# A ring of five half one-hots and four id fields in a recommender tower

## The reference, cut to what matters

```python
e = jnp.stack([tbl_0[ids[:, 0]], ..., tbl_25[ids[:, 25]]], axis=1)
combined = jnp.concatenate([dense[:, None, :], e], axis=1)          # 2048 x 27 x 128
inter = jnp.einsum('bfd,bgd->bfg', combined, combined)[:, iu, ju]   # pairs f < g
h = jnp.concatenate([dense, inter, dense], axis=1)
h = jnp.maximum(h @ W_top1 + b_top1, 0.0)     # 607 x 512
h = jnp.maximum(h @ W_top2 + b_top2, 0.0)     # 512 x 256
y = h @ W_top3                                # 256 x 1
```

## Time and profile before

| what | value |
|---|---|
| median of three runs | 360.73 us |
| the profiled execution | 359.68 us |
| its span on the core | 357.9 us |
| TensorE matmuls busy | 324.8 us (91%) |
| VectorE busy | 240.9 us (67%) |
| ScalarE busy | 183.4 us (51%) |
| GpSimd busy | 250.5 us (70%) |
| granted TensorE clock, mean | 0.986 |

### The profile page before, as it was taken

One profiled execution on the slowest core, in us unless ns is written; L12 is line 12 of the kernel. 1 busy time (PEld: TensorE's weight loads), 2 busy tenths in 40 slices (PEclk: granted clock), 3 DMA queues, 4 the chain that ended last, 5 costly groups with the idle time before them and its releaser, 6 DMA issues.

```text
span 357.9 us, 10386 instructions
## 1 busy us (share of the span) xinstructions
PE 324.8 (91%) x4192; PEld 312.4 (87%) x4192; DVE 240.9 (67%) x721; ACT 183.4 (51%) x359; POOL 250.5 (70%) x268
## 2 busy tenths in 40 slices
PE   0565779999999999999999999999999999998966
PEld 0464679999999999999899999999899999997955
DVE  3999976996479663995299555986199547941011
ACT  2345455457534763557544664457345763376224
POOL 4777777777777777777777777777777777774310
PEclk9999989999999999999999999999999999999889
DMA  7999577573457424652456344642466335521220
GB/s 184 259 233 228 139 218 198 121 192 82 98 110 192 95 75 107 162 145 71 100 124 183 88 97 98 164 132 70 104 142 170 77 103 108 123 66 38 43 69 0
DMA packets 47470, 44.80 MB, mean 125 GB/s; under 512 B 26139, under 2 KB 41499, under 8 KB 47423
## 3 DMA queue, kind: packets, MB, share of 16 engines
q1 hardware_dynamic: 37946, 25.90, 30.4%
q0 software_dynamic: 8448, 17.04, 19.3%
q10 hardware_dynamic: 1028, 1.20, 1.2%
HBM read 39.33 MB, written 4.78 MB: 123 GB/s over the span
## 4 chain that ended last, share of the span: by engine, by line
PE 56%; POOL 18%; DVE 9%; DMA 7%; issue 7%; SPq 1%; ACT 1%; ACTq 0%
PE ps_o L330 28%; POOL rows L309 18%; PE ps_m L367 10%; PE ps_g L356 9%; DVE onehot L719 6%; PE ps_t L341 5%; DVE tbl_lo L704 3%; DMA oh_ids<-onehot_ids 2%; PE ps_m L395 1%; DMA x<-interaction_scratch 1%; DMA interaction_scratch<-inter 1%; DMA b2s<-b 1%; DMA x<-w_pairs 1%; DMA rows<-tables,idx 1%; PE ps_o L410 1%
## 5 line engine op out<-in xcount | busy, mean ns | idle before, releaser
L309 POOL DMA_INDIRECT rows<-tables,idx x256 | 245.6, 959 | 81.5 <-issue 76.5
L719 DVE TENSOR_SCALAR onehot<-oh_ids,rownum 125x256 fp32r<-125x256 int32 x640 | 200.4, 388 | 51.7 <-PE ps_o L330 46.6
L330 PE MATMUL ps_o<-onehot,tbl_hi 125*128 125x256 f32 x640 | 160.5, 291 | 22.5 <-DVE tbl_lo L704 22.0
L330 PE MATMUL ps_o<-onehot,tbl_lo 125*128 125x256 f32 x640 | 156.3, 284 | 0.0
L330 PEld LDWEIGHTS ps_o<-onehot,tbl_hi 125*128 125x128 f32 x640 | 123.3, 193 | 27.1 <-DVE tbl_lo L704 23.9
L330 PEld LDWEIGHTS ps_o<-onehot,tbl_lo 125*128 125x128 f32 x640 | 123.7, 193 | 0.0
L533 ACT ACTIVATE emb<-ps_o 128x256 f32<-128x256 f32 x80 | 49.3, 740 | 90.0 <-PE ps_o L330 86.9
L356 PEld LDWEIGHTS ps_g<-emb 128*54 128x54 f32 x2048 | 56.6, 136 | 4.9 <-issue 2.6
L356 PE MATMUL ps_g<-emb 128*54 128x54 f32 x2048 | 58.9, 220 | 2.0 <-issue 1.3
L549 ACT ACTIVATE emb<-ps_t 128x512 f32<-128x512 f32 x64 | 46.4, 727 | 8.2 <-PE ps_t L341 7.9
L564 ACT ACTIVATE inter<-ps_g 128x432 f32<-128x432 f32 x64 | 34.0, 531 | 18.5 <-PE ps_g L356 16.4
(11 more groups left out here) (55 smaller groups left out, 207.5 us busy)
## 6 DMA issues: line engine op xcount, KB each, us to landing
oh_ids<-onehot_ids SPq DMA_DIRECT2D x80, 128.0 KB
rows<-tables,idx POOLq DMA_INDIRECT x256
x<-interaction_scratch SPq DMA_DIRECT2D x24, 117.0 KB
inter<-small_tables SPq DMA_DIRECT2D x4, 448.0 KB
interaction_scratch<-inter SPq DMA_DIRECT2D x30, 47.2 KB
interaction_scratch<-inter SPq DMA_DIRECT2D x28, 42.2 KB
interaction_scratch<-inter SPq DMA_DIRECT2D x30, 38.2 KB
dense<-dense_e SPq DMA_DIRECT2D x8, 128.0 KB
```

The lines of the kernel that those rows point to most:

```text
L309: pool.indirect_dma_start(rows[e][:, k, :], None, tables[k], bass.IndirectOffsetOnAxis(ap=idx[:, NG * hh + k:NG * hh + k + 1], axis=0),).t ...
L330: mm = pe.matmul(o, tbl[p][:, k, c, :], onehot[n % SLOTS_OH][:, c, :], start=(c + p == 0), stop=(c == TCHUNKS - 1 and p == 1))
L719: op = nc.vector.tensor_scalar(onehot[n % SLOTS_OH][:, c, :], oh_ids[0:TPART, n % IDS, :], rownum[:, c:c + 1], None, ALU.is_equal)
```

## The change

The three whole one-hots become a ring of five half one-hots (`RING = 5`): half `g = 2n + c // PART` lies in slot `g % 5`. VectorE waits before each half until `onehot_used` is at least `g - 4`, that is until the half five places earlier is used; before it was the half six places earlier. The id slots go from six to four, so `load_ids(n)` waits for one-hot `n-4` instead of `n-6`. SP's list is changed with it: in the first block `load_ids(n)` stands behind `load_stage(n)` where it was `load_ids(n+2)`, and for each later block fields 0 to 6 are asked for ahead and fields 7, 8 and 9 between the stores and `load_x`; before it was fields 0 to 8 ahead and field 9 there.

```diff
-    SLOTS_OH = 3
-    IDS = 6
+    RING = 5
+    IDS = 4
...
-        onehot = [sb(f"onehot{s}", [TPART, TCHUNKS, BLOCK], f32r) for s in range(SLOTS_OH)]
+        onehot = [sb(f"onehot{s}", [TPART, PART, BLOCK], f32r) for s in range(RING)]
...
                 store_wrapped(sp, i, range(QUAD), inter_stored)
-                load_ids(NO * (i + 1) + NO - 1)
+                for n in range(7, NO):
+                    load_ids(NO * (i + 1) + n)
                 for c in range(PAIR_CHUNKS):
                     load_x(sp, i, c)
...
             load_dense(0)
-            load_ids(4)
-            load_ids(5)
-            load_stage(sp, 4)
-            load_ids(6)
             load_idx(1, 2 * NG, HALVES * NG)
-            for n in range(5, NO):
+            for n in range(4, NO):
                 load_stage(sp, n)
-                load_ids(n + 2)
+                load_ids(n)
             load_dense(1)
             for n in range(NO, ITEMS):
                 load_stage(sp, n)
-                load_ids(n + 2)
+                load_ids(n)
...
-            for n in range(ITEMS + 2, 2 * NO - 1):
+            for n in range(ITEMS, NO + 7):
                 load_ids(n)
...
-                    for n in range(NO * (i + 1), NO * (i + 2) - 1):
+                    for n in range(NO * (i + 1), NO * (i + 1) + 7):
                         load_ids(n)
...
# lookup (TensorE)
+                    g = 2 * n + c // PART
-                        pe.wait_ge(onehot_ready, 2 * n + c // PART + 1)
+                        pe.wait_ge(onehot_ready, g + 1)
-                        mm = pe.matmul(o, tbl[p][:, k, c, :], onehot[n % SLOTS_OH][:, c, :],
+                        mm = pe.matmul(o, tbl[p][:, k, c, :], onehot[g % RING][:, c % PART, :],
...
# make_onehot (VectorE)
+                    g = 2 * n + c // PART
-                        wait(dve, onehot_used, 2 * (n - SLOTS_OH) + c // PART + 1)
-                    op = nc.vector.tensor_scalar(onehot[n % SLOTS_OH][:, c, :], oh_ids[0:TPART, n % IDS, :],
+                        wait(dve, onehot_used, g - RING + 1)
+                    op = nc.vector.tensor_scalar(onehot[g % RING][:, c % PART, :], oh_ids[0:TPART, n % IDS, :],
```

## The result

The changed kernel takes a median of 384.67 us (four runs, 383.64 to 386.43) against 360.22 for the kernel before: 1.069 times as long, 95% interval 1.063 to 1.074. The profiled execution took 386.43 us, with a span of 384.6 where it was 357.9: 26.7 us more. It is the slowest of the four.

The account below looks back on a forecast made before the run. TensorE was taken to bound blocks 1 to 6, GpSimd's fixed gather pace as second bound. Terms 2.6 (first block), 2.3 (block 1), 13.2 (blocks 2 to 7) sum to 18.1, less 0.8: 17.3 on 359.68, 377.0 us; range 363 to 387.

Parts of the forecast that it names:

- the chain: Blocks 2 to 7: ring delays one-hot 2, SP's stores wait behind field 6's ids, field 7's ids come late; 13.2 us.
- the free 0.8: At the end TensorE is ready about 0.8 us before the last gather; that much delay is free, subtracted from the sum.
- The ids' landing: Field 7's ids, behind the stores, land 2.7 us after issue; VectorE stalls 2.03 us in a block like 2.
- rival 4: The landing is late, 3.6 us or a little more: stall 2.9 to 3.6, 383 to 387 us; chance 0.12.
- The ring in the blocks: Blocks like 2: 60 chunks left after TensorE's first half lookup; by itself some 0.04 us a block, whole margin gone.
- Block 1: Block 1: restart 60.99, field 7's ids land at 74.6, wanted at 74.0; end 82.15 against 79.87, 2.3 us.
- The ring in the first block: First block: second one-hot halves wait for lookups; 1.05 us at one-hot 2 plus 1.5, all 2.6 reach block 1.
- The seven of 0.22: First block, one-hots 3 to 9: VectorE's fifth chunk 0.22 us late each, seven times, 1.5 us.
- The first block's ids: First 10 us: two id loads of 128 KB leave; gain 0, at most 0.1 us.
- rival 2: The clock falls too after TensorE's waits, 1.7 us lost seven times: 12 more, 389 us; chance 0.10.
- rival 3: GpSimd's pace hides the loss, gathers end at 327.5 whatever TensorE does; time stays 359.7 us; chance 0.07.

Follow-up runs that it names:

- two moves in SP's list and two in VectorE's: Changed kernel with field 6's load behind eighth store, first block's ids ahead of tables, split_lo(k) between one-hot halves, dense weight split before one-hot 12's ring wait: 359.69 us.

## Why the prediction was right, and where its terms were off
The direction, the place and the chain were right: 377.0 was forecast, 384.67 came, inside the range of 363 to 387. The rows show each link, and the chain was cut by experiments in three places (which one-hot the load waits for, where it stands, when field 7's ids are issued).

The sum was too small in every stretch of the kernel. In the profiled execution 17.3 us were forecast and 26.7 came: 4.5 for 2.6 at the start of block 1, 3.1 for 2.3 in block 1, 16.7 for 11.0 in blocks 2 to 6, and 2.5 for 1.4 in block 7 with the tail (2.2 less the free 0.8).

**The ids' landing** was the largest error of size. I took 2.7 us from the stores; the id loads of blocks 2 to 7 behind the stores took 3.3 to 3.8 (3.57 in block 2). The row that I took it from the earlier trace rows is of four stores in the tail that GpSimd issues; the trace has no landing of a store from SP's queue, so the price came from another queue. Four stores of `L197`, also issued by GpSimd in the tail, took 3.0 to 4.4 us. That is rival 4 (0.12; 383 to 387 us), the forecast's mechanism with the landing of the upper rows, and the time that came lies in its range. In part that is luck: 7 of the missing 9.4 us are in blocks 2 to 7, the rest is other terms. Issue was forecast 11.9 us after the block's first lookup and was 11.5 to 12.8, later in some blocks. So the stall was 2.6 to 4.0 us and not 2.0. "DMA: Bandwidth & Descriptors" of the Trainium skill ("Anatomy of one DMA") would have made it 2.3, an estimate by a fit for DMAs issued from GpSimd; the trace does not agree for SP's, and says 3.3 or more for this load in this place.

**The ring in the blocks** was right for blocks 2 to 4: with the ring alone they are 39.4 to 39.6 us. Blocks 5 and 6 of that run were 40.8 and 40.3, through waits for gathered rows of which the prediction knew nothing.

**Block 1** was forecast 2.3 us longer and was 3.1. VectorE waited 1.08 us for ids and not 0.7, and restarted 1.58 us after the block's start, for 1.33 before. I had also put the time at which lookup 9's ninth matmul is wanted at 79.87; it starts at 79.71. The wait of SP's dense load for the dense weights was not in my reckoning at all; it decides once field 6 is out of the way.

**The ring in the first block** was too dear: 2.6 forecast, 0.7 to 1.0 measured in VectorE's list. The wait at one-hot 2 was there (0.98 for 1.05). The seven of 0.22 were not: VectorE's eight chunks take 2.64 us with the short ring and took 2.63 before. I reckoned its fifth chunk from the mean pace, though the row itself was longer than eight such paces; the chunks already had a pause of about that size in these places. What makes that pause was not tried.

**The first block's ids** failed as a step. I wrote that two loads leave the first 10 us and costed the rest at nothing. But fields 4 to 13 were also moved further back among the table loads (`load_ids(n)` behind table n, where it was `load_ids(n + 2)`), and I did not ask when they land. They landed too late four times:

```profile
37.67 2.54 DVE L718 TENSOR_SCALAR onehot<-oh_ids,rownum 125x256 fp32r<-125x256 int32 x8 [0.54 <-DMA oh_ids<-onehot_ids]
...
49.52 2.54 DVE L718 TENSOR_SCALAR onehot<-oh_ids,rownum 125x256 fp32r<-125x256 int32 x8 [3.41 <-DMA oh_ids<-onehot_ids]
```

The last row, field 0 of block 1, comes partly in place of a wait of 1.64 us for weights. By the first weight split the list is 3.6 us behind, and the bias load that releases block 1 landed after 5.57 us where it took 3.75: 4.5 us in all. So the 2.6 for the start of block 1 had one term too large and one missing; the surplus of the one covered part of the other by luck.

**The clock** (rival 2, 0.10) came true in part. I held that the wait would be spread over six halves; it is one wait at lookup 7's first half, as VectorE makes the later halves almost as fast as TensorE wants them. After 1.32 to 1.6 us of it the clock stayed (blocks 2, 4, 6), after 1.90 and 2.4 it fell (blocks 3, 5, 7), with 0.83 granted in the 10 us around it. The length of the wait does not decide it alone: in the run with the ids ahead of the tables it stayed after 2.14 us and fell after 1.92. "TensorE: Matmul & The Clock Gate" ("HAM oscillation") of the Trainium skill describes such rounds, and the trace agrees in every second block. (Block 1's 0.96 follows a wait of 2.4 us for the biases at its start.) The price was not 1.7 us but what a block has beyond VectorE's wait: 43.41 - 39.42 - 3.2 = 0.8 in block 3, 43.82 - 39.42 - 3.9 = 0.5 in block 5.

**Not slower** (rival 3) is out: the 0.8 us of waiting for the last gather was used up. But its premise, that the gathers end at 327.5 whatever TensorE does, did not hold: the last one started 3.1 us later in the changed kernel and 5.4 later with the ring alone.

## What to carry to other kernels
A queue that issues DMAs in order is a lock: shrinking a buffer is cheap or dear by what stands behind the load that now waits, and by who consumes the last thing in that list. Two cuts that cost 3.5 us each can cost 24 together, when one makes an event late and the other puts an urgent transfer behind it. Before shrinking a ring, list for every slot wait the event that frees it, and move from behind it what does not need it; here two moves in SP's list and two in VectorE's gave all of it back. Taking away the wait that decides can bring up the next one in the same list: here the dense load's, which had been almost hidden behind field 6's.

## What was not expected of the hardware
The same 128 KB id load took 2.9 to 7.7 us to land where the trace has it, and was never as quick as the median (2.6) of the four stores of `L188` that GpSimd issues in the tail; 7.5 and 7.7 were behind table loads in the first block. In the changed kernel the clock stayed after waits of up to 1.6 us and fell after 1.90 and more, but another run has a wait of 2.14 us that left it at full rate. Twelve fillers of 1.60 us in the wait kept it at full rate, with 0.96 us still waited.
